# Causal attention of a four-layer hybrid block: from whole-array score matmuls with a centred softmax to 32-row head tiles whose scores are computed twice

## What is computed

```python
qkv = x @ w_qkv.T                                  # x: layer-normed tokens, [16, 256, 128]
scores = jnp.einsum('bhqd,bhkd->bhqk', q, k) * scale          # scale = 1/sqrt(16)
scores = jnp.where(causal[None, None], scores, -jnp.inf)
attn = jax.nn.softmax(scores, axis=-1)
out = jnp.einsum('bhqk,bhkd->bhqd', attn, v)
return out.transpose(0, 2, 1, 3).reshape(b, t, d) @ w_out.T   # and t = t + this
```

## Time and profile before

| what | value |
|---|---|
| median of 3 runs | 1610.93 us (1606.83 to 1615.15) |
| the profiled execution, its own time | 1611.11 us |
| its span in the trace | 1609.4 us |
| PE busy | 1183.4 us (74%) |
| DVE busy | 928.7 us (58%) |
| ACT busy | 676.1 us (42%) |
| POOL busy | 595.8 us (37%) |
| causal attention in the trace | from about 955.6 us (first set-up instructions) to 1277.0 us (last statistics) |

### The profile page before, as it was taken

The page is one execution under the profiler, slowest core; times in us unless marked ns, Lnnn a source line. Parts: engine busy times, 40 slices in busy tenths (PEclk is TensorE's granted clock), DMA queues, the critical chain, the costliest instruction groups (busy, mean ns, idle before and its releaser), DMA issues. The chain is left out here.

```text
span 1609.4 us, 30797 instructions
## 1 busy us (share of the span) xinstructions
PE 1183.4 (74%) x8969; PEld 960.6 (60%) x9000; DVE 928.7 (58%) x2702; ACT 676.1 (42%) x1493; POOL 595.8 (37%) x705
## 2 busy tenths in 40 slices
PE   4468869888977656749999927899999740079992
PEld 3367434545666544449999925677777640078991
DVE  7654986625687355325555548776767550056774
ACT  3422745645555324436666612333333310055651
POOL 5500340355645205723434322021112007746660
PEclk9679989999999757869999967999999755589995
DMA  2279011000000251111111121000000201112225
GB/s 71 52 118 155 16 41 26 13 12 8 9 2 2 80 236 46 53 38 47 49 46 47 44 81 40 1 1 0 0 0 0 85 34 53 53 49 60 65 59 162
DMA packets 91143, 78.60 MB, mean 49 GB/s; under 512 B 21808, under 2 KB 84016, under 8 KB 89776
## 3 DMA queue, kind: packets, MB, share of 16 engines
q1 hardware_dynamic: 81072, 56.98, 13.7%
q0 software_dynamic: 9984, 20.53, 3.8%
HBM read 44.29 MB, written 33.18 MB: 48 GB/s over the span
## 5 line engine op out<-in xcount | busy, mean ns | idle before, releaser
L1785 PE MATMUL m_eps_up<-m_ext,m_w_up 128*128 128x128 f32 x1856 | 238.2, 279 | 1.1 <-DVE m_w_up L1832 0.7
L1751 POOL DMA_INDIRECT ys_scratch<-m_yout,m_xin x152 | 159.1, 1047 | 204.1 <-DVE m_yout L1853 149.4
L1785 PEld LDWEIGHTS m_eps_up<-m_ext,m_w_up 128*128 128x128 f32 x1856 | 222.2, 194 | 4.4 <-issue 2.0
L1806 ACT ACTIVATE m_w_up<-m_up 128x512 f32 x152 | 95.8, 630 | 193.5 <-PEq L1578 142.2
L1606 POOL DMA_INDIRECT xs_scratch<-m_xn,m_slot x128 | 122.8, 959 | 114.9 <-POOLq L1373 44.1
L1795 PE MATMUL m_eps_y<-m_w_down,m_ht 128*128 128x128 f32 x1216 | 161.4, 276 | 0.6 <-DVE m_ht L1845 0.5
L1795 PEld LDWEIGHTS m_eps_y<-m_w_down,m_ht 128*128 128x128 f32 x1216 | 148.7, 193 | 1.0 <-DVE m_ht L1845 0.7
L1775 PE MATMUL m_eps_x<-ident,m_xin 128*128 128x128 f32 x152 | 44.1, 291 | 139.6 <-DMA m_xin<-xs_scratch 139.2
L2060 POOL TENSOR_TENSOR c_kx<-c_k,head 128x2048 f32<-128x2048 f32 x16 | 57.6, 3603 | 229.4 <-ACT c_k L2083 229.4
L2087 ACT ACTIVATE c_e<-c_e 128x512 f32<-128x512 f32 x96 | 60.4, 630 | 187.3 <-DVE c_e L2136 187.3
L1826 DVE COPY m_ext<-m_eps_x 128x128 f32<-128x128 f32 x152 | 42.7, 281 | 129.3 <-PE m_eps_x L1775 126.9
(11 more groups left out here) (317 smaller groups left out, 2607.1 us busy)
## 6 DMA issues: line engine op xcount, KB each, us to landing
xs_scratch<-empty SPq DMA_DIRECT2D x20, 516.0 KB, 11.1
m_xin<-xs_scratch SPq DMA_DIRECT2D x152, 64.5 KB, 1.8
m_y<-ys_scratch SPq DMA_DIRECT2D x22, 256.0 KB, 5.2
m_up<-in_m_gate SPq DMA_DIRECT2D x2, 2048.0 KB, 14.4
m_up<-in_m_up SPq DMA_DIRECT2D x2, 2048.0 KB, 19.2
m_down<-in_m_down SPq DMA_DIRECT2D x2, 2048.0 KB, 23.7
a_q_in<-q_scratch SPq DMA_DIRECT2D x80, 32.0 KB, 1.7
c_rows<-ys_scratch SPq DMA_DIRECT2D x10, 256.0 KB, 3.1
```

The costliest lines, as they stand in the source:

```text
L1751: pool.indirect_dma_start(ys_dram, bass.IndirectOffsetOnAxis(xin[:, u, C:C + 1].bitcast(U32), 0), yout[:, u, :], None).then_inc(stored[u], 16)
L1785: last = pe.matmul(ps[u % 2][:, k * P:(k + 1) * P], w[:, u % 2, k * P:(k + 1) * P], xt[:, u % 2, :], start=True, stop=True)
L1806: act.activation(w_up[0][:, u % 2, :], m.up[0][:, e, :], ACT.Copy).then_inc(placed[0], 1)
```

## The change

The attention is written anew. What it does now:

- **Layout.** The projection weights are spread by POOL once (`wide`), so that each head of q and k lies in a 32-row strip of its own (16 values, the 17th row free, the rest zero), four heads (QUADS) to a half, two halves. There is no `kx` and no `spread`. One unit is two heads with all their 384 allowed score columns (128 queries x 128 keys, and 128 x 256); four units per image.
- **First scores** (`score`): mask over 384 columns for each of the two heads, then four matmuls with 32 contraction rows, the two heads in different row strips and different PSUM banks (`ps_s` is one tile of two banks, so there is one buffer for units). DVE only takes the maxima (`top_of`), two reductions per unit, straight into the place of the 17th row. `turn_peak` transposes the peaks of an image into `ps_q`; `lower` adds them to q, and k has -1 in its 17th row (the bias `minus` in `k_copy`), so that q.k - peak comes out of a matmul.
- **Second scores** (`rescore`): the transposed scores, keys on partitions, minus the peak; ACT takes the exponential straight out of PSUM, 768 columns at once (`exp`). No mask here: POOL sets the forbidden triangle of the exponentials to zero, two `affine_select` over 128x2x128 per unit.
- **Weighing** (`weigh`): values (128 keys x 32 columns, with a one in column 17) are the weights, exponentials stream past, four heads into four 32-column strips. The output is turned: `drain` (ACT) copies it, `turn_back` transposes it to tokens on partitions, `o_norm` follows as before. `turn_e` and `back` are gone.
- **Order.** No hardware loop: for each image step i all engines have a straight list, in which the first scores of image i, the second scores of i-1 and the end of i-2 are interleaved. Late tokens are taken four per step in steps -1 to 3, after the maxima.

Core of the diff (long common parts left out):

```diff
-UN = 6
+SIDE = 32
+QUADS = P // SIDE
+HALVES = NH // QUADS
+UN = 4
+SPAN = T + P
+ETS = 4
...
+            for n in range(UN * B):
+                pool.wait_ge(exped, n + 1)
+                if n == 0:
+                    pool.wait_ge(widened, 3)
+                for at in (0, T):
+                    diagonal = e[:, n % ETS, :, at:at + P]
+                    pool.affine_select(out=diagonal, in_=diagonal, compare_op=ALU.is_ge, fill=0.0, base=0,
+                                       pattern=[[0, 2], [1, P]], channel_multiplier=-1).then_inc(cut, 1)
...
+            def exp(b, u):
+                n = UN * b + u
+                act.wait_ge(rescored, n + 1)
+                if n >= ETS:
+                    act.wait_ge(weighed, (n - ETS) // 2 + 1)
+                act.activation(e[:, n % ETS], ps_e[:, :, 0:SPAN], ACT.Exp, scale=float(HD) ** -0.5).then_inc(exped, 1)
...
+            def score(b, u):
+                half, pair = heads(u)
+                n = UN * b + u
+                if u == 0:
+                    pe.wait_ge(q_out, b + 1)
+                    pe.wait_ge(k_out, b + 1)
+                if n:
+                    pe.wait_ge(peaked, 2 * n)
+                for i in range(2):
+                    pe.matmul(ps_s[:, i, 0:SPAN], ident_b[:], mask[:].rearrange("p a b -> p (a b)"), start=True, stop=False)
+                for tile in range(2):
+                    for i, j in enumerate(pair):
+                        rows_of = slice(SIDE * j, SIDE * j + SIDE)
+                        at = P if tile else 0
+                        last = pe.matmul(ps_s[:, i, at:at + P * (tile + 1)], q[rows_of, b % 2, half, tile * P:(tile + 1) * P],
+                                         k_[rows_of, b % 3, half, 0:P * (tile + 1)], start=False, stop=(tile == 1))
+                last.then_inc(scored, 1)
...
+            def rescore(b, u):
...
+                for c in range(2):
+                    for i, j in enumerate(pair):
+                        rows_of = slice(SIDE * j, SIDE * j + SIDE)
+                        at = T if c else 0
+                        last = pe.matmul(ps_e[:, i, at:at + T - P * c], k_[rows_of, b % 3, half, c * P:(c + 1) * P],
+                                         qm[rows_of, b % 2, half, c * P:T], start=True, stop=True)
+                last.then_inc(rescored, 1)
+
+            def weigh(b, half):
+                pe.wait_ge(cut, 2 * (UN * b + 2 * half + 2))
...
+                for c in range(2):
+                    for j in range(QUADS):
+                        n = UN * b + 2 * half + j // 2
+                        at = T if c else 0
+                        last = pe.matmul(ps_o[SIDE * j:SIDE * (j + 1), half * T + c * P:(half + 1) * T],
+                                         vx[:, b % 3, c, QUADS * half + j, :], e[:, n % ETS, j % 2, at:at + T - P * c],
+                                         start=(c == 0), stop=(c == 1))
                 last.then_inc(weighed, 1)
...
+            for i in range(-2, B + 3):
+                now, before, last_but_one = 0 <= i < B, 0 <= i - 1 < B, 0 <= i - 2 < B
+                if now:
+                    score(i, 0)
+                if before:
+                    turn_peak(i - 1)
+                if last_but_one:
+                    weigh(i - 2, 1)
+                if now:
+                    score(i, 1)
+                if 0 <= i + 1 < B:
+                    turn_x(i + 1)
+                if before:
+                    rescore(i - 1, 0)
+                if last_but_one:
+                    turn_back(i - 2)
+                if now:
+                    score(i, 2)
+                if before:
+                    rescore(i - 1, 1)
+                if 0 <= i + 1 < B:
+                    project(i + 1)
+                if now:
+                    score(i, 3)
+                if before:
+                    rescore(i - 1, 2)
+                    weigh(i - 1, 0)
+                if last_but_one:
+                    turn_o(i - 2)
+                if before:
+                    rescore(i - 1, 3)
+                if last_but_one:
+                    project_o(i - 2)
```

More of the change, by code:

```diff
@@ L1943, in _ @@
             in_turn(act, B, 4, copy)
-UN = 6
[L1949 to L1974, removed]
 EARLY = 12
 LATE = NT - EARLY
+LATE_AT = 3
+SIDE = 32
[4 more added lines that the diff above has]
+ETS = 4
 def causal_attention(nc, top, wqk, wv, wout, m, ys_dram, keep):
@@ L2023, in causal_attention, with heads @@
         block = ctx.enter_context(nc.Block())
[L2025 to L2031, removed]
+        CONSTS = 11
+        def heads(u):
+            half, pair = divmod(u, 2)
+            return half, [2 * pair, 2 * pair + 1]
         @block.sync
@@ L2065, in _, with norm @@
         @block.scalar
         def _(act):
-            def norm(b, i, u, early):
-                if not early:
+            def norm(b):
+                if b >= 2:
                     act.wait_ge(turned, b - 1)
-                if isinstance(b, int) and b == EARLY // 2 - 1:
+                if b == EARLY // 2:
                     act.wait_ge(late_norm.ready, 1)
@@ L2213, in project @@
                 for h in range(2):
-                    last = pe.matmul(ps_v[:, h * C:(h + 1) * C], xt[:, u, h * P:(h + 1) * P], wv_s[:], start=True, stop=True)
+                    last = pe.matmul(ps_x[:, h * C:(h + 1) * C], xt[:, b % 2, h * P:(h + 1) * P], wv_s[:], start=True, stop=True)
                 last.then_inc(v_done, 1)
-            def score(b, i, u, early):
-                tile, h0, heads, keys = unit(i)
-                n = UN * b + i
-                if i == 0:
-                    pe.wait_ge(kx_ready, b + 1)
-                if not early or UN * b + i >= 2:
-                    pe.wait_ge(centred, n - 1)
-                pe.matmul(ps_s[i % 2][:], ident_b[:], mask[:, tile, :], start=True, stop=False)
-                pe.matmul(ps_s[i % 2][:], q[:, u, tile * P:(tile + 1) * P], kx[:, u, h0:h0 + heads, 0:keys],
-                          start=False, stop=True).then_inc(scored, 1)
@@ new lines, in turn_peak @@
+            def turn_peak(b):
+                pe.wait_ge(peaked, 2 * UN * (b + 1))
+                if b + 1 < B:
+                    pe.wait_ge(q_out, b + 2)
+                for half in range(HALVES):
+                    for tile in range(2):
+                        last = pe.transpose(ps_q[:, half * T + tile * P:half * T + (tile + 1) * P],
+                                            peak[:, b % 2, tile, half].rearrange("p j d -> p (j d)"), keep.ident[:])
+                last.then_inc(peak_turned, 1)
@@ new lines, in turn_back, with turn_o @@
+            def turn_back(b):
+                pe.wait_ge(drained, b + 1)
+                pe.wait_ge(k_out, min(b + 3, B))
+                for tile in range(2):
+                    for half in range(HALVES):
+                        at = (tile * HALVES + half) * P
+                        last = pe.transpose(ps_k[:, at:at + P], os[:, half, tile * P:(tile + 1) * P], keep.ident[:])
+                last.then_inc(back_turned, 1)
+            def turn_o(b):
+                pe.wait_ge(o_ready, b + 1)
+                if b + 3 < B:
+                    pe.wait_ge(v_out, b + 4)
+                elif b:
```

358 lines of the change are left out of this document (194 added, 164 removed).

## The result

The changed kernel takes **1553.88 us** (median of 4 runs, 1553.02 to 1554.75) against 1611.22 us before in the same session: ratio 0.9652, 95% interval 0.9623 to 0.9681, 57 us or 3.5% faster. The prediction was 1561 us, in a range of 1540 to 1597.

What follows compares the result with a forecast made beforehand. PE was taken to bound the attention: 13.7 us of work plus 0.9 of waits gave 14.6 per image against 17.65, 49 us over 16; with start and end, 1611.1 - 49.6 = 1561 us, range 1540 to 1597.

Steps and rivals of the forecast that it cites:

- The bound: Attention: PE bounds it, 16.8 of 17.65 us per image before; forecast 13.7 of work, 14.6 with waits.
- Row strips: First and second scores on PE: two strips nearly at once, 0.70 us per unit, 5.6 for eight units per image.
- the 1577 us worked out from it: Score units at 0.83 rather than 0.70 us, from the skill's 77%: step 1.0 us longer, whole kernel 1577.
- Waits: PE per image: the same 0.9 us of waits as before, added to 13.7 to give 14.6.
- Weighing, transposes, projections, changes of the cut: PE per image: weighing 1.3, transposes 1.4, q and k 1.7, v and output 0.9, 15 cut changes 1.5 us.
- Other engines: Costed at nothing, beside PE's work: per image DVE about 7.5 us, ACT 6.4, POOL 3.6.
- Start and end: Attention's ends: first score about 967.3, early images 8.5 us, end 18; last statistics at 1227.4, 49.6 us earlier.
- I take 8.5 exposed: Early images of the attention: late tokens on DVE, in one lump, expose 8.5 us in place of 10.4.
- Rival 1: Score units: weight loads of different row strips do not overlap, 0.9 us per unit, 26 in all, 1587 us; chance 0.14.
- Rival 2: Each image step: new wait from single score buffers or POOL, 1.0 us per image more, 1577 us; chance 0.12.
- Rival 3: Eight score units: row strips do not run together, 1.28 instead of 0.70 us each, 1635 us; chance 0.10.
- Rival 4: PE in the attention: clock falls to 1.2 GHz, over 25 us per image, beyond 1700 us if lasting; chance 0.03.

Runs made afterwards that it cites:

- e2: Changed kernel with first-score units in order 0, 1, 3, 2, so neighbouring first and second scores use the same strips; 1619.7 us, ratio to kernel before 0.973.
- e5: Changed kernel without POOL's selections, the weighing waiting for the exponentials instead, part of the computation left out; 1548.4 us, ratio to kernel before 0.962.
- e3: Changed kernel with turn_x moved behind unit 0's second scores, making a third place with four strips at once; 1591.5 us, ratio to kernel before 0.956.
- e4: Changed kernel without the mask matmuls of the first scores, POOL alone zeroing the triangle; 1585.9 us, ratio to kernel before 0.953.
- e9: Changed kernel with both heads of a unit in the same row strip, first scores only; 1613.6 us, ratio to kernel before 1.003.
- e10: Changed kernel with late tokens taken one behind each pair of maxima, the first four before v's copy; 1526.3 us, ratio to kernel before 0.949.
- e11: Changed kernel with late tokens spread, no mask matmuls and turn_x behind unit 0's second scores, full result; 1502.4 us, ratio to kernel before 0.934.

## Why the prediction was right, point by point

- **The bound.** PE bound the stage before and bounds it now; right. The forecast of what it would do per image held in kind, and the sum was 1.5 us too long (14.6, measured 13.11). The saving per image is 4.6 us where 3.05 was forecast. The period that was to show the forecast right, near 14.6, did not come; 13.11 is just above the 13 below which the prediction calls itself wrong.
- **Row strips.** "I take it as the nearest, with a little lost: 0.70." In e2 the first of two neighbouring units, entered from the whole array, takes 0.76 us, and the second, left for the whole array, 0.75; a unit alone, with both, takes 0.85. So entering and leaving cost about 0.1 us each, and the unit itself 0.65, which is two strips fully at once (0.64): 0.70 and 0.10 had been set. The inference from column strips to row strips was sound. But the list was read unit by unit: that neighbouring first and second scores lie in the other two strips, and so go four at a time, was overlooked. e2 prices it: **1.22 us per image**, the larger part of the error. The Trainium skill (TensorE: Matmul & The Clock Gate, Measured speedup vs the span model) gives 3.07 times for four row strips, 77% of the ideal. This trace agrees for four strips: 1536 columns fully at once would take 0.65 us, and the two places take 0.92 and 0.88, 0.82 and 0.78 without the 0.1 for leaving, so 79% and 83%. The prediction had put that figure on a pair, and the 1577 us worked out from it lay further from the result than the estimate from rows did.
- **Waits.** "With the same 0.9 us of waits" was the second error: in the steady part there are almost none (99.4 of 101 us busy). The prediction carried the term over without asking what the old waits were. The view of waits of the kernel before (PE alone, 1016.8 to 1265.9) names them:

```profile
PE c_ps_v L2265 <- ACT c_ot L2102: 12.7, 14, 1.0
```

That is 0.9 us per image, once: the output projection stood right behind the transposes of its own input and waited for the copy between them. In the new list a unit of second scores lies there (1112.99 to 1113.85), and the projection starts without a wait. Against these two errors, 2.1 us in all, the other terms came out 0.6 too low together.
- **Weighing, transposes, projections, changes of the cut.** 0.79 per half including a change (0.64 + 0.1 reckoned), peaks 0.59, q and k and v 2.27, mask 0.42 with its change (0.33 + 0.1): within 0.15 us each. The small excesses are on the same side: 0.05 for each of the four lone units and of the two weighings, 0.1 each for q, k and v together and for the output (0.54, 0.43 reckoned).
- **Other engines.** Exponential 810 ns (0.83 reckoned), maxima 425 and 682 (410 and 690), selection 408 (450). POOL off the path: shown by e5.
- **Start and end.** First score 12 us after entry, as forecast (11.7). "I take 8.5 exposed" is the term that failed the other way: the first five images take 88.0 us where five steady ones take 65.6, 22 us exposed. The lump was seen, not what it does: PE idles and then loses the clock. From the first score to the last statistics it is 253.3 us, so 21 are left for the end, 3 more than the 18 reckoned. The too long period (16 x 1.5 = 24 us) and these two (14 and 3 us too little) nearly cancelled. That 1561 lay within 7 us of 1554 is therefore luck in part; the bound and the strips were right, the sizes were not.
- **Rival 1**, weights bound the strips: no. The eight loads of a unit lie within 0.52 us (the row below), beside the matmuls; at 0.11 each one after another they would have taken 0.9. The 0.107 us per load of the Trainium skill (TensorE: Matmul & The Clock Gate, LDWEIGHTS) may hold for one load; eight of them one after another would be 0.86, longer than the 0.52 measured here, so loads of different row strips overlap.

```profile
1101.70 0.52 PEld L2262 LDWEIGHTS c_ps_s<-c_k,c_q 32*128 32x128 f32 x8 [0.32 <-issue]
```

- **Rival 2**: not in the steady part of the change, but there once the list is shortened: 0.30 us before the first scores (e3), and 0.32 from the single buffer of second scores (e4).
- **Rival 3**, strips one after another: its price per unit was right (0.65 measured in e9 for 0.58 to 0.64), its condition didn't hold.
- **Rival 4**, the clock: 1.00 in the steady part, as the earlier trace rows suggested; but 0.75 over the first five images (0.93 with the late tiles spread in e10), from gaps, not from strips.

## What to carry to other kernels

When a matmul fills only 16 or 32 rows or columns of the array, give each head a strip of its own and put groups that lie in different strips next to each other in the list, across stages too; the order inside a group is free. Then look at what a lump of small work on another engine does to a single-buffered ring: here the sums of 20 late token tiles, moved but not made fewer, were worth 24 us, and of the 20 us that two windows show, 8 went with TensorE's clock. If another engine already zeroes what a mask forbids, and a maximum over the forbidden values is still an upper bound, the mask in front of it can go too. Before a wait of the old kernel is carried into a forecast, find out which one it is: the new order may fill it.

## What the runs showed that was not expected

- In the session in which the kernel before takes 1665 us instead of 1611, this attention is entered 50 us later and the time in it is the same. It is not the chip: e10 and e11 ran on the one of that session, with 1609 us for the kernel before. Why the earlier stages were slower there was not looked into.
